# Cross-attention and a mixture-of-experts FFN on one core: the shared FFN of the last five token groups in steps of its own

## The chip, the cores and the metric

One core of one Trainium2 chip runs one program. The metric is the device time in microseconds of one execution of it; lower is better. The time before is 1953.99 us, the median of 3 runs (1952.19 to 1956.04).

## What is computed

```python
# x: 16 x 1024 tokens of 512; context: 16 x 64 x 384; 8 heads of 64; all float32, FFN weights bfloat16
x = x + attention(layernorm(x), ctx) @ Wo + bo           # softmax over 64 context rows, 8 heads
X = layernorm(x).reshape(16384, 512)
scores = sigmoid(X @ gate_w.T)                           # 32 experts
idx = top_k(scores + bias, 4)                            # 4 experts for each token
w = scores[idx] / sum(scores[idx])
# each expert takes its first 512 tokens in order of the tokens; a token beyond is dropped there
ye = (silu(xe @ W1) * (xe @ W3)) @ W2                    # for each expert
out = sum of w * ye over the token's experts
out = out + silu(X @ sw1.T) * (X @ sw3.T) @ sw2.T        # the shared FFN, for every token
x = x + out
```

## The kernel before

The program has two blocks, one after the other, with all five engines joined between them.

**The first block** (`set_up_and_tokens`, L118) goes once over the 16384 tokens, as 128 tiles of 128 tokens. Four tiles are a group (32 groups, numbers 0 to 31). It is one software pipeline written out by hand: every engine runs `step(n)` for n = 0 to 147 (`STEPS`, L56), and each piece of work has a lag (L53 to L55) that says in which step a tile or a group comes to it. The engines meet only through semaphores. For tile t the stages are:

- `XT_LOAD` (n = t+6) and `XT_SPLIT` (t+7): the turned input is loaded and split into a high and a low part, so that products are near float32 (ScalarE L579, GpSimd L658).
- `SCORES` (t+8): TensorE makes the scores of all heads with 12 matmuls into `S_ps` (L374). VectorE takes the maximum (L911) and subtracts it (L917), ScalarE does the exponential (L593), VectorE the sums (L933, L940), GpSimd the division (L664). The scores of the last tile are in step 135.
- `MIX` (t+9): TensorE turns the probabilities (L491), ScalarE and VectorE split them (L585, L924), TensorE makes 12 matmuls into `O_ps` (L390).
- `X1` (t+10): VectorE adds `O_ps` to the tokens (L877) and takes the statistics for the second layernorm. `roots` (L696) is a chain of 13 small VectorE operations (Newton's iteration for 1/sqrt) in each even step, for two tiles at a time.
- `X2` (t+13): ScalarE makes the normalized rows (L568) and their high part in float16 (L573), VectorE the low part (L904), and the SP queue stores the rows and turns both parts with two DMA transposes (L339, L344). `x2_h` and `x2_l` are one buffer each, so the next tile's rows wait until the turned ones have landed (L572, L903).
- `LOGITS` (t+14): 8 small matmuls (L407).

For a group g the stages are `ROUTE` (n = 4g+17, sigmoid and the best 4), `MEMBERS` (4g+18, and on TensorE the ranks, L432), `SLOTS_AT` (4g+19, the slot numbers), `WEIGHTS` (4g+20), `W_STORE` (4g+21). The shared FFN takes `FFN_UP` (4g+17 and 4g+18) and `FFN_DOWN` (4g+19 and 4g+20). An up half c is 16 matmuls into `G_ps` and `U_ps` (L417), a tanh (L619), the gate and the product on VectorE (L754, L759), the high part on ScalarE (L622) and the low part on GpSimd (L651). A down part j is 8 matmuls into the same two banks (L427) and two additions on VectorE (L764). There is one tile `hid` and one pair `ht_h`, `ht_l`.

`TABLE` (n = t+20): GpSimd files the tokens of a tile in the table of slots, with four indirect DMAs (L640) on its own queue, two before and two after its split of `xt` (L653, L660). The second block reads that table, so it can't begin before the last is filed.

```python
file(at(n, TABLE), 0, 2)        # L653
...                             # xt_l (L658)
file(at(n, TABLE), 2, TOP)      # L660
```

Five groups of tokens are held on the chip at a time (`XRING`); the SP queue stores a pair of tiles once its down part is done (L328).

**The second block** (`experts`, L1013) goes over the 32 experts: GpSimd gathers rows by the table (L1087), TensorE turns them and makes the expert's FFN, and GpSimd adds the weighted results into the output (L1099). The change doesn't touch it.

## Time and profile before

| | |
|---|---|
| median of 3 runs | 1953.99 us (1952.19 to 1956.04) |
| the profiled execution | 1951.55 us, its span 1949.7 us |
| first block (to the first instruction of the second) | 1468.38 us |
| second block | 481.3 us |
| TensorE matmuls, weight loads | busy 90% and 64% of the span |
| VectorE, ScalarE, GpSimd | busy 82%, 38%, 64% |

A row of the timeline gives the start in us from the span's start, the duration in us, the engine, the line, the operation, what it writes and reads, and in brackets how long the engine sat idle before it and what released it. The ends of matmuls are modelled. `xr` is the tokens' tile, `x_h` and `x_l` stand for `x2_h` and `x2_l`.

### The profile page before, as it was taken

To read this page: it belongs to the slowest core of one execution; us is meant where nothing else is said; L and a number is where in the kernel's file an instruction comes from. 1 tells how busy PE (TensorE), PEld (TensorE's weight loads), DVE (VectorE), ACT (ScalarE), POOL (GpSimd) and SP (SyncE) were. 2 spreads that over 40 slices of the span, in tenths; PEclk is the share of its full clock that TensorE was granted. 3 is DMA by queue.
4 is the path that set the end of the run, shared out by engine and by line. 5 is a ranking of instruction groups with operands and counts; after the bars stand their busy time and mean duration, and the time that the engine had idled before them with its cause. 6 is when DMAs were issued, how large, how long until landed. Compare 5 with 4: busy or idle time off the path is not lost. (4 is left out here: it accounts for less than half of the span.)

```text
span 1949.7 us, 31394 instructions
## 1 busy us (share of the span) xinstructions
PE 1747.2 (90%) x9424; PEld 1243.4 (64%) x9424; DVE 1591.0 (82%) x4143; ACT 748.8 (38%) x1253; POOL 1241.8 (64%) x1107
## 2 busy tenths in 40 slices
PE   6898899999999999999999999999732999999991
PEld 4775567777777767777776777776411556555551
DVE  5887789999999999999999999999821777676671
ACT  3343334444444444344443444443301444444440
POOL 2235566666676666667666666666675577888864
PEclk8998999999999999999999999999975999999995
DMA  7339987764446464444545444554326799999976
GB/s 210 99 103 101 100 131 131 127 142 119 118 125 145 118 140 132 118 116 132 141 121 139 122 119 121 130 139 111 91 55 204 171 232 218 226 232 220 226 140 78
DMA packets 335195, 275.00 MB, mean 141 GB/s; under 512 B 199858, under 2 KB 242098, under 8 KB 335028
## 3 DMA queue, kind: packets, MB, share of 16 engines
q1 hardware_dynamic: 289972, 203.48, 44.0%
q0 software_dynamic: 45056, 69.52, 18.6%
q8 instruction: 77, 1.26, 0.3%
q14 instruction: 90, 0.74, 0.2%
HBM read 134.07 MB, written 105.25 MB: 123 GB/s over the span
## 5 line engine op out<-in xcount | busy, mean ns | idle before, releaser
L640 POOL DMA_INDIRECT slot_table<-tok,slot x512 | 514.9, 1006 | 125.7 <-issue 121.1
L658 POOL TENSOR_TENSOR xt_l<-xt,xt_h 128x512 fp32r<-128x512 f32 x128 | 166.1, 1298 | 181.8 <-PE S_ps L374 118.5
L1099 POOL DMA_INDIRECT out<-ye,idx x128 | 205.2, 1603 | 88.4 <-issue 37.2
L390 PE MATMUL O_ps<-m_h,pt_h 128*128 128x512 f32 x512 | 217.7, 425 | 33.7 <-issue 30.8
L1251 DVE TENSOR_TENSOR xe_l<-TE_ps,xe_h 128x512 f16<-128x512 f32 x128 | 88.4, 691 | 168.5 <-issue 87.3
L374 PE MATMUL S_ps<-a_h,xt_h 128*128 128x512 f32 x512 | 200.9, 392 | 7.2 <-POOL xt_l L658 7.2
L390 PE MATMUL O_ps<-m_h,pt_l 128*128 128x512 f32 x512 | 201.3, 393 | 0.0
L374 PE MATMUL S_ps<-a_h,xt_l 128*128 128x512 f32 x512 | 201.1, 393 | 0.0
L374 PE MATMUL S_ps<-a_l,xt_h 128*128 128x512 f32 x512 | 200.6, 392 | 0.0
L390 PE MATMUL O_ps<-m_l,pt_h 128*128 128x512 f32 x512 | 200.2, 391 | 0.0
L651 POOL TENSOR_TENSOR ht_l<-hid,ht_h 128x512 fp32r<-128x512 f32 x64 | 82.8, 1294 | 181.2 <-ACT ht_h L622 181.1
L664 POOL TENSOR_TENSOR prob<-prob,rsum 128x512 f32<-128x512 f32 x128 | 134.5, 1051 | 69.0 <-DVE rsum L940 62.1
L593 ACT ACTIVATE prob<-S_ps,rs 128x512 f32<-128x512 f32 x128 | 88.0, 687 | 230.1 <-DVE S_ps L917 211.2
L1087 POOL DMA_INDIRECT rows<-x2aug,idx x128 | 133.4, 1042 | 43.4 <-issue 37.8
L390 PEld LDWEIGHTS O_ps<-m_h,pt_h 128*128 128x128 f32 x512 | 96.5, 188 | 73.5 <-issue 56.2
L585 ACT ACTIVATE pt_h<-TP_ps 128x512 fp32r<-128x512 f32 x128 | 75.9, 593 | 166.0 <-PE TP_ps L491 142.7
L877 DVE TENSOR_TENSOR xr<-xr,O_ps 128x512 f32<-128x512 f32 x128 | 87.1, 681 | 61.2 <-PE O_ps L390 50.9
L622 ACT ACTIVATE ht_h<-hid 128x512 fp32r<-128x512 f32 x64 | 40.5, 633 | 248.4 <-DVE hid L759 245.9
L568 ACT ACTIVATE x<-xr,nb,rs 128x512 f32<-128x512 f32 x128 | 103.5, 809 | 81.9 <-DVE nb L726 59.2
L1151 PE MATMUL TE_ps<-ident_r,rows 128*128 128x128 f32 x512 | 71.0, 265 | 67.0 <-DMA rows<-x2aug,idx 53.9
L1151 PEld LDWEIGHTS TE_ps<-ident_r,rows 128*128 128x128 f32 x512 | 58.6, 145 | 91.8 <-issue 57.5
L374 PEld LDWEIGHTS S_ps<-a_h,xt_h 128*128 128x128 f32 x512 | 97.1, 190 | 29.1 <-issue 6.1
(175 smaller groups left out, 4837.6 us busy)
## 6 DMA issues: line engine op xcount, KB each, us to landing
xt<-in_xT SPq DMA_DIRECT2D x128, 256.0 KB
xr<-in_x SPq DMA_DIRECT2D x64, 512.0 KB, 3.9
x2aug<-x SPq DMA_DIRECT2D x128, 256.0 KB
out<-xr SPq DMA_DIRECT2D x64, 512.0 KB
up_w<-in_w SPq DMA_DIRECT2D x64, 256.0 KB
slot_table<-tok,slot POOLq DMA_INDIRECT x512
down_raw<-in_w SPq DMA_DIRECT2D x32, 256.0 KB
x2t_h<-x_h SPq DMA_TRANSPOSE x128
```

The lines of the kernel that those rows point to most:

```text
L374: last = pe.matmul(S_ps[:, :], left[:, kc, :], right[:, b % 2, kc, :], start=(m == 0), stop=(m == 3 * KD - 1))
L390: last = pe.matmul(O_ps[:, :], left[:, p * P:(p + 1) * P], right[:, b % 2, p, :], start=(m == 0), stop=(m == 3 * PAIRS - 1))
L568: act.activation(x2[:, t % 2, :], x_tile(t), ACT.Identity, bias=nb2[:, q % 2, t % 2:t % 2 + 1], scale=rs[:, (q + LATER) % 2, 1, t % 2:t % ...
L593: act.activation(prob[:, t % 2, :, :], S_ps[:, :].rearrange("p (h j) -> p h j", h=H), ACT.Exp, scale=rs[:, q % 2, 0, t % 2:t % 2 + 1]).the ...
L640: pool.indirect_dma_start(table, bass.IndirectOffsetOnAxis(ap=slot[:, g % 2, i, q:q + 1], axis=0), tok[:, t:t + 1], None, bounds_check=SLO ...
L658: pool.tensor_tensor(xt_l[:, :, :], xt[:, :, :], xt_h[:, t % 2, :, :].bitcast(F32), ALU.subtract).then_inc(xt_lo, 1)
L664: pool.tensor_tensor(prob[:, t % 2, :, :], prob[:, t % 2, :, :], rsum[:, :].unsqueeze(2).to_broadcast([P, H, SKV]), ALU.mult).then_inc(pro ...
L877: dve.tensor_tensor(x_tile(s10), x_tile(s10), O_ps[:, :], ALU.add).then_inc(x1_done, 1)
L1087: pool.indirect_dma_start(rows[:, r, c, :].bitcast(F32), None, x2aug, bass.IndirectOffsetOnAxis(ap=idx[:, e, c:c + 1], axis=0), bounds_che ...
L1099: pool.indirect_dma_start(out, bass.IndirectOffsetOnAxis(ap=idx[:, e, c:c + 1], axis=0), ye[:, e % 4, c, :], None, bounds_check=TOKENS + P ...
L1151: last = pe.transpose(TE_ps[i % 2][:, kc * P:(kc + 1) * P].bitcast(F32R), rows[:, e % RING, i, kc * P:(kc + 1) * P], ident_r[:, :])
L1251: dve.tensor_tensor(xe_l[dst], TE_ps[i % 2][:, :].rearrange("p (c t) -> p c t", c=KD), xe_h[dst], ALU.subtract).then_inc(t_lo, 1)
```

## The change

Nothing of the computation changes. What changes is the step and the place in which pieces are done.

- The shared FFN of groups 27 to 31 (`HELD` = 27) is done in steps 136 to 147, in an order written as a table (`shared_at`). For these groups the low part of the hidden values is made on VectorE (`hidden_lo`), not on GpSimd.
- Rows (`rows_at`): tiles 122 and 123 both in step 135, 124 and 125 in step 137, 126 and 127 in step 138 (before: one tile in each of steps 135 to 140). From tile 125 on an odd tile uses the space of `xt` for its parts. There are two semaphores for the turned parts, by the tile's parity. Logits (`logits_at`): tiles 122 and 123 in step 136, the last four in step 139.
- The last roots are done in step 137 (before 138).
- Routing (`routed_at`): group 29 as before, group 30 one step sooner, group 31 two steps sooner. Filing (`filed_at`): tiles 120 to 127 two in a step, in steps 139 to 142 (before 140 to 147).
- The turned rows of groups 29 to 31 go into the space of `wqc`, `wo_sb`, and `kbd` with `vbd`, which are no longer read by then.
- From step 136 on VectorE runs `late_step`, an order of its own.

```diff
+LAST = TILES - 4
+HELD = GROUPS - 5
+STEPS = LAST + 25
+def rows_at(n):
+    if n < LAST + X2 - 2:
+        return [n - X2] if n >= X2 else []
+    return {LAST + 11: [LAST - 2, LAST - 1], LAST + 13: [LAST, LAST + 1], LAST + 14: [LAST + 2, LAST + 3]}.get(n, [])
+def logits_at(n):
+    if n < LAST + 14:
+        return rows_at(n - 1)
+    return [LAST, LAST + 1, LAST + 2, LAST + 3] if n == LAST + 15 else []
+def filed_at(n):
+    t = n - TABLE
+    normal = [t] if 0 <= t < LAST - 4 else []
+    pair = 2 * (n - LAST - 15)
+    return normal + ([LAST - 4 + pair, LAST - 3 + pair] if 0 <= pair < 8 else [])
+def routed_at(n, lag):
+    for sooner in range(3):
+        g = GROUPS - 3 + sooner
+        if n == 4 * g + lag - sooner:
+            return g
+    g = group_at(n, lag)
+    return g if g is not None and g < GROUPS - 2 else None
+def shared_at(n):
+    if n < LAST + 12:
+        up = [("up", g, c) for c in range(2) for g in (group_at(n, FFN_UP + c),) if g is not None and g < HELD]
+        down = [("down", g, j) for j in range(2) for g in (group_at(n, FFN_DOWN + j),) if g is not None and g < HELD]
+        return up + down
+    u, d, g = "up", "down", HELD
+    return {12: [(u, g, 0)], 13: [(u, g, 1)], 14: [(u, g + 1, 0), (d, g, 0)], 15: [(d, g, 1), (u, g + 1, 1)],
+            16: [(u, g + 2, 0)], 17: [(d, g + 1, 0), (d, g + 1, 1)], 18: [(u, g + 2, 1)],
+            19: [(u, g + 3, 0), (d, g + 2, 0), (d, g + 2, 1)], 20: [(u, g + 3, 1), (u, g + 4, 0)],
+            21: [(d, g + 3, 0), (d, g + 3, 1)], 22: [(u, g + 4, 1)], 23: [(d, g + 4, 0), (d, g + 4, 1)]}.get(n - LAST, [])
...
# TensorE
+                    late = n > LAST + 12
+                    for k, (kind, g, part) in enumerate(shared_at(n)):
+                        if kind == "up":
+                            shared_up(g, part)
+                        else:
+                            shared_down(g, part)
+                        if late and k == 0:
+                            for t in logits_at(n):
+                                logits(t)
+                            if routed_at(n, MEMBERS) is not None:
+                                rank(routed_at(n, MEMBERS))
...
# ScalarE
+                        act.wait_ge(x2_done, t + 1)
+                        after(act, x2_lo, t - 1)
+                        if t == LAST + 1:
+                            act.wait_ge(xt_lo, TILES)
+                        elif t > LAST:
+                            act.wait_ge(x2_turned[t % 2], q * 32)
+                        elif t:
+                            act.wait_ge(x2_turned[(t - 1) % 2], ((t - 1) // 2 + 1) * 32)
+                        act.activation(row_parts(t)[0], x2[:, t % 2, :], ACT.Copy).then_inc(x2_hi, 1)
...
+                    for kind, g, c in shared_at(n):
+                        if kind == "up":
+                            if c and g > HELD:
+                                hidden_hi(g, 0)
+                            act.wait_ge(g_done, TURN_OF["up", g, c] + 1)
                             after(act, ht_lo, g * 2 + c)
                             act.activation(hid[:, :], G_ps[:, :], ACT.Tanh, scale=0.5).then_inc(th_done, 1)
+                            if c or g <= HELD:
+                                hidden_hi(g, c)
...
# GpSimd
+                    for kind, g, c in shared_at(n - 1):
+                        if kind == "up" and g < HELD:
...
# VectorE
+                def late_step(n):
...
+                    if members is not None:
+                        route_mark(members)
+                        route_count(members)
+                        route_before(members)
+                        route_member(members)
+                    for t in rows_at(n):
+                        rows_lo(t)
+                    if slots is not None:
+                        slot_place(slots)
+                        slot_spread(slots)
+                        slot_list(slots)
+                    if weights is not None:
+                        for k in range(5):
+                            weigh_ops(weights, k)
+                    if s10 is not None:
...
+                    for k in range(NEWTON + 1):
+                        if n == LAST + 12:
+                            roots(n, k)
+                        elif n == LAST + 13:
+                            roots(n + 1, k)
+                    if members is not None and members < GROUPS - 1:
+                        slot_over(members)
+                        slot_rank(members)
+                    for kind, g, k in pieces[:1]:
+                        shared_piece(kind, g, k)
+                    if early is not None:
...
+                    if members == GROUPS - 1:
+                        slot_over(members)
+                        slot_rank(members)
+                    for kind, g, k in pieces[1:]:
+                        shared_piece(kind, g, k)
```

## Rows read from the trace of the kernel before

**Rows 1.** The page: the span in 40 equal slices, tenths (busy; granted clock)

```profile
PE   6898899999999999999999999999732999999991
PEclk8998999999999999999999999999975999999995
```

**Rows 2.** Windows: the eleven steps up to 1376.74, and the tail of the block

```profile
1274.00:1376.74 102.74, 97.81 (x516) 70.67 (x515) 99.01 (x279) 39.64 (x68) 68.94 (x63) 0.98 0.43 113
1376.74:1461.40 84.66, 43.43 (x218) 25.25 (x217) 41.89 (x143) 15.58 (x26) 58.86 (x58) 0.81 0.34 78
```

The columns of rows 2 are the window, its length, then busy us (and instructions) of TensorE's matmuls, its weight loads, VectorE, ScalarE and GpSimd, the granted clock, the share of the DMA engines and GB/s.

**Rows 3.** Timeline of GpSimd: filings and what interrupts them, from step 136 on

```profile
1384.61 0.99 POOL L640 DMA_INDIRECT slot_table<-tok,slot  x1 [0.17 <-issue]
...
1401.67 1.26 POOL L651 TENSOR_TENSOR ht_l<-hid,ht_h 128x512 fp32r<-128x512 f32 x1 [7.10 <-ACT ht_h L622]
...
1409.42 1.45 POOL L640 DMA_INDIRECT slot_table<-tok,slot  x1 [0.16 <-issue]
...
1428.32 1.27 POOL L651 TENSOR_TENSOR ht_l<-hid,ht_h 128x512 fp32r<-128x512 f32 x1 [3.34 <-ACT ht_h L622]
...
1460.44 0.98 POOL L640 DMA_INDIRECT slot_table<-tok,slot  x1 [0.30 <-issue]
1468.38 0.20 POOL L1112 MEMSET ident_f<- 128x128 f32 x1 [6.96 <-POOLq L270]
```

**Rows 4.** Timeline of VectorE: step 125's first operation; from step 134 to 136

```profile
1273.08 0.68 DVE L877 TENSOR_TENSOR xr<-xr,O_ps 128x512 f32<-128x512 f32 x1
...
1365.17 0.67 DVE L877 TENSOR_TENSOR xr<-xr,O_ps 128x512 f32<-128x512 f32 x1
...
1365.76 1.04 DVE L713 TENSOR_SCALAR nt<-mv 128x4 f32<-128x4 f32 x1
...
1375.07 0.15 DVE L721 SCALAR_TENSOR_TENSOR nt<-nt 128x4 f32<-128x4 f32 x1
...
1376.74 0.68 DVE L877 TENSOR_TENSOR xr<-xr,O_ps 128x512 f32<-128x512 f32 x1
1377.33 1.15 DVE L851 SCALAR_TENSOR_TENSOR over<-taken,member 128x128 f32<-128x128 f32 x1
...
1379.85 0.69 DVE L911 TENSOR_REDUCE top_s<-S_ps 128x8 f32<-128x512 f32 x1
...
1384.98 0.69 DVE L877 TENSOR_TENSOR xr<-xr,O_ps 128x512 f32<-128x512 f32 x1 [0.21 <-PE O_ps L390]
```

**Rows 5.** Timeline of GpSimd: its low parts of the hidden values beside those steps

```profile
1365.47 1.29 POOL L651 TENSOR_TENSOR ht_l<-hid,ht_h 128x512 fp32r<-128x512 f32 x1 [3.22 <-ACT ht_h L622]
...
1377.04 1.29 POOL L651 TENSOR_TENSOR ht_l<-hid,ht_h 128x512 fp32r<-128x512 f32 x1 [2.52 <-ACT ht_h L622]
```

**Rows 6.** Timeline of ScalarE: the high parts of two tiles, one after the other

```profile
1408.65 0.63 ACT L573 ACTIVATE x_h<-x 128x512 f16<-128x512 f32 x1
...
1413.15 0.63 ACT L573 ACTIVATE x_h<-x 128x512 f16<-128x512 f32 x1 [3.17 <-DMA x2t_l<-x_l]
```

**Rows 7.** Timeline of TensorE: an up half's first matmuls into each bank; a down part's

```profile
1400.52 0.59 PE L417 MATMUL G_ps<-x2t_h,up_sb 128*128 128x512 f16 x1
...
1403.89 0.63 PE L417 MATMUL U_ps<-x2t_h,up_sb 128*128 128x512 f16 x1
...
1413.33 0.48 PE L427 MATMUL G_ps<-down_sb,ht_h 128*128 128x512 f32 x1
...
1414.35 0.39 PE L427 MATMUL U_ps<-down_sb,ht_h 128*128 128x512 f32 x1
```

**Rows 8.** Timeline of VectorE: a long wait in step 137, then the last group's operations

```profile
1396.52 0.69 DVE L877 TENSOR_TENSOR xr<-xr,O_ps 128x512 f32<-128x512 f32 x1 [5.15 <-remote]
...
1430.31 0.69 DVE L754 SCALAR_TENSOR_TENSOR hid<-hid,G_ps 128x512 f32<-128x512 f32 x1 [0.54 <-ACT hid L619]
1431.11 0.69 DVE L759 TENSOR_TENSOR hid<-hid,U_ps 128x512 f32<-128x512 f32 x1
...
1442.21 0.68 DVE L764 SCALAR_TENSOR_TENSOR xr<-U_ps,xr 128x512 f32<-128x512 f32 x1
```

More of the change, by code:

```diff
@@ L322, in step @@
                             load_context(bp)
-                    for k in range(2):
-                        g = group_at(n, OUT + k)
-                        if g is not None:
-                            sp.wait_ge(g_free, g * 4 + 3 + k)
-                            sp.wait_ge(u_free, g * 4 + 3 + k)
+                    for kind, g, k in shared_at(n - 1):
+                        if kind == "down":
+                            sp.wait_ge(g_free, TURN_OF[kind, g, k] + 1)
+                            sp.wait_ge(u_free, TURN_OF[kind, g, k] + 1)
                             sp.dma_start(out_pairs[2 * g + k], x_pair(g, k)).then_inc(out_stored[g % XRING][k], 16)
@@ L502, in step @@
                         turn_probs(t)
[L503 to L505 removed]
+                    late = n > LAST + 12
+                    if not late:
+                        for t in logits_at(n):
+                            logits(t)
                     bp, q = kv_job(n)
@@ L529, in step @@
                         prep_chunk(b, j)
-                    g = group_at(n, MEMBERS)
-                    if g is not None:
+                    g = routed_at(n, MEMBERS)
+                    if g is not None and not late:
                         rank(g)
@@ new lines, in shared_piece @@
+                def shared_piece(kind, g, k):
+                    if kind == "up":
+                        if k and g > HELD:
+                            hidden_lo(g, 0)
+                        gate(g, k)
+                        hidden(g, k)
+                        if k or g == HELD:
+                            hidden_lo(g, k)
+                    else:
+                        residual(g, k, G_ps, g_done, g_free)
+                        residual(g, k, U_ps, u_done, u_free)
+                def late_step(n):
+                    s9, s10 = at(n, MIX), at(n, X1)
+                    early, members = routed_at(n, ROUTE), routed_at(n, MEMBERS)
+                    slots, weights = routed_at(n, SLOTS_AT), routed_at(n, WEIGHTS)
+                    pieces = shared_at(n)
+                    if members is not None:
[3 more added lines that the diff above has]
+                        route_member(members)
+                    for t in rows_at(n):
+                        rows_lo(t)
[7 more added lines that the diff above has]
+                    if s10 is not None:
+                        dve.wait_ge(o_done, s10 + 1)
+                        dve.tensor_tensor(x_tile(s10), x_tile(s10), O_ps[:, :], ALU.add).then_inc(x1_done, 1)
+                        dve.wait_ge(x1_done, s10 + 1)
+                        after(dve, agg2, s10 - 3)
+                        dve.bn_stats(st2[:, s10 % 4, :], x_tile(s10)).then_inc(bn2, 1)
+                        aggregate2(s10)
+                    if s9 is not None:
+                        dve.wait_ge(pt_hi, s9 + 1)
+                        dve.tensor_tensor(pt_l[:, :], TP_ps[:, :], pt_h[:, :].bitcast(F32), ALU.subtract).then_inc(pt_lo, 1)
+                    for k in range(NEWTON + 1):
[9 more added lines that the diff above has]
+                    if early is not None:
+                        route_scores(early)
+                        route_sigmoid(early)
+                        route_bias(early)
+                        route_best(early)
+                        route_cut(early)
+                    if members == GROUPS - 1:
[3 more added lines that the diff above has]
+                        shared_piece(kind, g, k)
@@ L871, in step @@
                     heads = S_ps[:, :].rearrange("p (h j) -> p h j", h=H)
-                    up = [group_at(n, FFN_UP + c) for c in range(2)]
-                    down = [group_at(n, FFN_DOWN + j) for j in range(2)]
+                    pieces = shared_at(n)
                     if s10 is not None:
@@ L947, in step @@
                         route_scores(early)
-                    for c in range(2):
-                        if up[c] is not None:
-                            gate(up[c], c)
                     roots(n, 10)
-                    for j in range(2):
-                        if down[j] is not None:
-                            residual(down[j], j, G_ps, g_done, g_free)
+                    for kind, g, k in pieces[:1]:
+                        if kind == "up":
+                            gate(g, k)
+                        else:
+                            residual(g, k, G_ps, g_done, g_free)
                     roots(n, 11)
@@ L962, in step @@
                         route_bias(early)
-                    for c in range(2):
-                        if up[c] is not None:
-                            hidden(up[c], c)
-                    for j in range(2):
-                        if down[j] is not None:
-                            residual(down[j], j, U_ps, u_done, u_free)
+                    for kind, g, k in pieces[:1]:
+                        if kind == "up":
+                            hidden(g, k)
+                        else:
+                            residual(g, k, U_ps, u_done, u_free)
                     if early is not None:
```

159 lines of the change are left out of this document (88 added, 71 removed).

## The prediction

> **What bounds the kernel now.** I read the page's slices first [rows 1]: TensorE is busy at nine tenths in nearly all slices of the token pass, then falls to 7, 3 and 2 tenths around 1370 to 1500 us, with a lower granted clock. That dip is the only place where work can be filled in. The windows split it [rows 2]: in the steps before 1376.74 VectorE is busy 99.0 of 102.7 us and TensorE 97.8, so both are full; in the tail of the block TensorE has 43 us of work in 85 and VectorE 42. In the tail GpSimd is the engine that ends last [rows 3]: from 1384.61, the start of step 136, it issues 48 filings (L640, 12 tiles of four), one each 0.98 + 0.30 = 1.28 us, and the last starts at 1460.44. The second block begins at 1468.38, 6.96 us after it ended. 48 filings are 61.4 us of 76.8. The rest is four low parts of the hidden values (L651) with their handoffs, 5.0 us, and the waits before two of them, 7.10 and 3.34 us. So before the change the shared FFN costs twice: it fills full steps, and it holds up the filing.
>
> I count from the addition L877 that opens step 135 on VectorE, 1376.74 [rows 4]. Before, filing starts at +7.9, the last filing ends at +84.7 and the second block begins at +91.6.
>
> **Part 1: six up halves and five down parts leave steps 125 to 135.** Each half or part is two large VectorE operations; such an operation takes 0.69 us and the next starts 0.60 after it [rows 4], so 1.2 us of VectorE. TensorE loses more (3.4 us in an up step), but VectorE is the fuller one, so VectorE's share counts. There is a second term. In step 134 the small L713 takes 1.04 us and ends at 1366.80, just when GpSimd's L651 (1365.47 + 1.29) ends; a small operation of that chain otherwise takes 0.15 [rows 4, 5]. L851 of step 135 takes 1.15 and ends by the same 0.15 after the next L651. Without L651 I count back 0.9 for each. By kind of step:
> - first up half (125, 129, 133): 1.2 each, 3.6.
> - second up half (126, 130, 134): 1.2 + 0.9, but in 126 only 0.4 of the wait, 5.8 together.
> - first down part (127, 131): the next addition then waits for `O_ps`, as before step 136 (idle 0.21, rows 4), so the 1.2 is not won; only the 0.9 of L851 is: 1.7.
> - second down part (128, 132): the same loop leaves 0.9 of 1.2: 1.8.
>
> Sum to the start of step 135: 12.9 us of 103.7 (1273.08 to 1376.74, rows 4). Bounds: 0 if the loop scores, maximum, split, mix sets every step, 30 if TensorE did (six times 3.4 and five times 2.04, from two banks of a down part at 1.02 each, rows 7). I take 12.9, since VectorE has hardly a gap in these rows.
>
> **Part 2: step 135 gets two tiles of rows.** Both halves of tile 122 must be turned before `x_h` of tile 123 may be written, and from one to the next is 4.5 us [rows 6]. VectorE has L904 of tile 123 ahead of its maximum (L911), and behind that queue the exponential, the sums and GpSimd's last division, after which the filing starts. `x_h` of 122 at +0.4, of 123 at +5.0, L904 at +5.7, so L911 at +6.3 instead of +3.1 [rows 4]. L851's gain is spent in it. Filing starts at +10.7 instead of +7.9.
>
> **Part 3: the filing.** L651 is gone, but the slots must be ready. Group 29's 16 filings run from +10.7 to +31.2. Group 30's slots come in step 138. VectorE's queue by then, in its order (large operation 0.6, or 0.8 where the next depends on it [rows 8]; a copy on ScalarE 0.63 [rows 6]; a link of the roots about 0.2): weights, x1, statistics and the last split done at +13.8, roots +16.3, group 27's first half with its own low part +19.2, routing of 30 +21.5, members +23.1, rows 124 and 125 +25.0 (one waits for the other's low part), x1 +25.7, statistics +26.8, last roots +29.4, slots over +30.1, second half of 27 +32.9, rows 126 and 127 +35.8, slots of 30 at +37.0. GpSimd idles 5.8 us there and files group 30 until +57.5. Group 31's slots: the four last tiles are turned by about +40.5, logits +42.6, routing +45.4, members +51.1, slots +54.5, in time. Filing ends at +78, where it was +84.7.
>
> **Part 4: the held FFN.** It now goes through one `hid` and one `ht` pair, and this is what I expect to be late next. Group 28's low part is done at +49.6. Group 29 takes until +63.5, since it shares VectorE with group 31's members, slots and weights (4.9 us). After that a group costs 11.2 us: tanh and gate 1.4, four banks of down part at 1.02 [rows 7] 4.1, high and low part 1.4, then the second half's tanh, gate, product, high and low part 4.3. So low parts end at +74.7 and +85.9; the last two down parts with their additions end at +90.8. Before, the last addition ended at 1442.9, +66.2 [rows 8], beside the filing and hidden by it. TensorE's work from group 28's first half on is 8 up halves of 3.4 us and 10 down parts of 2.04, 48 us in 60, so it is not the limit while the clock is high.
>
> **Part 5: the joining of the blocks.** The last store must land and the engines meet. Before that took 6.96 us from the end of the last filing [rows 3], its landing included. For a store of the SP queue no row separates landing and joining; the bounds are 2 and 7, and I take 5.2, nearer to the row. The second block begins at +96.0, against +91.6: 4.4 us later.
>
> **Edits at nothing.** The split semaphore for turned rows, the moved order of gate and roots(10), and the table of turns change neither order nor count of the work before step 125. The stores of five groups (ten of 512 KB) pass in the tail, where the DMA share is 0.34 [rows 2]; if they didn't, the last store would add a few us to part 5. The other buffers are free by step 128.
>
> **Sum.** 12.9 gained, 4.4 given back, and 1 us for TensorE's first matmuls after its longest gap (about 6 us, +24 to +31): after gaps it starts at the lower level, 1.2 GHz, where a bank takes 3.37 us [rows 7], twice what it takes at 2.4. Net 7.5 us. The profiled execution took 1951.55, the median is 1953.99, 2.4 higher; from the median the forecast is 1946.5 us.
>
> **One wait of before is open.** VectorE sat idle 5.15 us in step 137 with nothing named as releaser [rows 8], in a stretch where every engine stood still, and GpSimd's wait of 7.10 holds it. My times of after are without such a wait. If it comes again it costs up to 5 us, so the forecast's own range reaches to 1951.
>
> **Rivals.**
> - *The filing sets the end.* Then FFN handoffs are shorter than I have them and the block ends at +78 + 7.0 = +85, 6.6 us sooner than before: 19.5 us gained, 1934.5. For it: filing was the bound before. Against: it needs the last FFN piece done by about +80, 11 us sooner than worked out. Chance 0.14. One filing of the tail took 1.45 us in place of 0.98 [rows 3]; ten such would change nothing in the forecast. The Trainium skill (SBUF — State Buffer, section SBUF: two separate sides) says that VectorE and GpSimd take a shared port pair as an exclusive lock, and that descriptors of GpSimd's own DMAs wait behind some VectorE operations; by that rule ten low parts moved to VectorE could hold ten filings by 0.69 each, the filing would end near +85, and this rival's time would be 1941.5.
> - *The steps give back only half.* The loop or GpSimd would bound the steps of 9.1 us that I expect (103.7 - 12.9 over ten); GpSimd has four filings, 5.1, and two operations of up to 1.3 in each, 7.7: half of 12.9 gained, 5.4 lost, 1.1 net, 1953. Chance 0.14.
> - *Slower: TensorE at the lower level in the tail.* The mean granted clock of the tail was 0.81 [rows 2], and up halves ran at 3.37 us a bank after gaps of 3 to 5 us. It now hangs on the path that ends last. With all of the 48 us doubled it takes 96 us in a window of 60, 36 us more; with half of it doubled 24 more work against 12 of slack, 12 us more: 1958.5. It turns the sign once more than about 40% of the held matmuls run at 1.2 GHz. Against: the gaps that I work out after +40 are near 2 us at most. Chance 0.12.
> - The forecast as worked out, 1942 to 1951: 0.60.
>
> **Numbers.** 0.2% (3.9 us) is about what a measurement of this kernel can tell from no change; below 1950.1 is faster, above 1957.9 slower. Faster: 0.57 of the forecast's 0.60, 0.14 of the first rival, 0.04 of the second: 0.75. Slower: 0.08 of the clock rival, 0.02 of the second: 0.10. Same: the rest, 0.15. Range 1936 to 1955: it takes in most of both mild rivals and leaves out the filing at its best and the clock at its worst.
>
> **What would show it.** Right: L877 of step 125 to L877 of step 135 about 91 us; a gap of some 5 us on GpSimd between its filings 16 and 17; L651's place taken by a VectorE operation; the last addition L764 some 12 us after the last filing; the second block beginning near 1460. Wrong: steps 126 to 134 as long as before (part 1), the last filing within 5 us of the last addition (part 4), TensorE's held matmuls at 0.63 us (the clock), or a change in the first 1270 us or in the second block's 481 us.

## The result, and the profile after

| | us | |
|---|---|---|
| before, median of 4 runs | 1953.76 | 1952.19 to 1956.04 |
| after, median of 4 runs | 1980.44 | 1977.12 to 1983.44 |
| after / before | 1.0138 | 95% interval 1.0118 to 1.0157 |
| forecast | 1946.5 | 1936 to 1955 |

The changed kernel is 26.7 us slower where 7.5 us faster was forecast. The profiled execution took 1980.39 us, its span 1978.6.

The page of the changed kernel, same two lines as [rows 1]:

```profile
PE   6898899999999999999999999977563999999991
PEclk8999999999999999999999999998886999999996
```

The dip of TensorE around the end of the first block has become wider, five slices at seven tenths or less where there were three. The windows of steps 125 to 134 and of the tail, to the last addition (columns as in [rows 2]):

```profile
1273.75:1368.41 94.66, 74.98 (x384) 58.63 (x384) 83.81 (x260) 36.10 (x60) 63.97 (x61) 0.93 0.40 101
1368.41:1496.83 128.42, 77.89 (x352) 41.33 (x350) 63.88 (x172) 20.65 (x35) 50.56 (x51) 0.84 0.22 62
```

The ten steps did get shorter: 94.7 us, where they took 103.7 [rows 4]. The tail ate it up: in 128 us TensorE has 78 us of work, VectorE 64, GpSimd 51. No engine is the bound. VectorE's timeline (the openings of steps 125, 135, 136 and 137, and the last addition of the held chain):

```profile
1273.75 0.68 DVE L1041 TENSOR_TENSOR xr<-xr,O_ps 128x512 f32<-128x512 f32 x1
...
1368.41 0.69 DVE L1041 TENSOR_TENSOR xr<-xr,O_ps 128x512 f32<-128x512 f32 x1 [1.28 <-issue]
...
1381.89 0.69 DVE L1002 TENSOR_TENSOR xr<-xr,O_ps 128x512 f32<-128x512 f32 x1 [1.88 <-issue]
...
1405.87 0.68 DVE L1002 TENSOR_TENSOR xr<-xr,O_ps 128x512 f32<-128x512 f32 x1
...
1496.14 0.69 DVE L856 SCALAR_TENSOR_TENSOR xr<-U_ps,xr 128x512 f32<-128x512 f32 x1 [0.23 <-PE U_ps L497]
```

GpSimd's timeline (the two gaps in which its filings wait for the slots of the next group, the last filing, the second block; compare [rows 3]). The 48 filings fall into runs of 14, 18 and 16: step 139 also files tiles 120 and 121 of group 30, and their first filings stand ahead of the last two of tile 119.

```profile
1418.17 0.98 POOL L726 DMA_INDIRECT slot_table<-tok,slot  x1 [21.53 <-DVE slot L956]
...
1454.30 0.98 POOL L726 DMA_INDIRECT slot_table<-tok,slot  x1 [13.23 <-DVE slot L956]
...
1474.00 0.98 POOL L726 DMA_INDIRECT slot_table<-tok,slot  x1 [0.30 <-issue]
1500.24 0.21 POOL L1275 MEMSET ident_f<- 128x128 f32 x1 [25.26 <-POOLq L338]
```

Counted from the opening of step 135, as in the prediction, the last addition ends at +128.4 and the second block begins at +131.8. The balance of the two profiled executions: 9.0 us gained in the steps, 0.7 lost before them, 131.8 - 91.6 = 40.2 lost in the tail, 3.0 gained in the second block (478.36 for 481.32): 28.9 us, the difference of the spans.

What the engines waited for is in the list of waits (waiting engine, tile and line, releaser: us in total, times, longest), here those that end on nothing that the profile names:

```profile
ACT lexp L688 <- remote: 28.1, 2, 22.2
ACT hid L708 <- remote: 11.7, 3, 4.9
ACT ht_h L625 <- remote: 11.0, 1, 11.0
DVE hid L846 <- remote: 5.4, 2, 3.7
DVE xr L856 <- remote: 5.0, 3, 2.8
```

All of these wait, directly or one step further, for TensorE. Its timeline, and below it ScalarE's, show how late its work is seen. The last logits matmul of group 31 is recorded from 1422.82 to 1423.00, the up half behind it to 1429.48; the exponential that needs nothing but the logits starts at 1438.18, and the tanh of that up half at 1443.85. TensorE, which waits for the gate behind that tanh, stands idle for 15.75 us. That up half is slow itself: it takes 6.6 us, with gaps that the profile puts to nothing (one of 1.04 us is shown), where it takes 3.6 us on chip C below. So TensorE's own stream of matmuls is disturbed in such a stretch too, and not only what the others see of it.

```profile
1422.82 0.18 PE L477 MATMUL R_ps<-gate_sb,vbd 128*128 128x32 bf16 x1
...
1425.39 0.38 PE L487 MATMUL G_ps<-x2t_l,up_sb 128*128 128x512 f16 x1 [1.04 <-issue]
...
1429.10 0.38 PE L487 MATMUL U_ps<-x2t_l,up_sb 128*128 128x512 f16 x1
1445.22 1.03 PE L487 MATMUL G_ps<-wqc,up_sb 128*128 128x512 f16 x2 [15.75 <-DVE hid L841]
```

```profile
1388.88 0.28 ACT L688 ACTIVATE lexp<-R_ps 128x128 f32<-128x128 f32 x1 [5.96 <-remote]
1393.81 0.60 ACT L708 ACTIVATE hid<-G_ps 128x512 f32<-128x512 f32 x1 [4.65 <-remote]
...
1438.18 0.28 ACT L688 ACTIVATE lexp<-R_ps 128x128 f32<-128x128 f32 x1 [22.17 <-remote]
...
1443.85 0.60 ACT L708 ACTIVATE hid<-G_ps 128x512 f32<-128x512 f32 x1 [4.87 <-remote]
```

I call this a late signal: the time from the recorded end of a matmul to the moment at which another engine goes on. There are three such stretches, 1383 to 1399, 1423 to 1444 and 1464 to 1477. In all but the last 2 to 3 us of each GpSimd files without a break, one filing about every 1.28 us. No wait of this kind begins where it doesn't file (1396.6 to 1418.2, 1441.1 to 1454.3, after 1475.0), and the last wait of each stretch ends 2.1, 2.8 and 2.1 us after the run of filings. The Trainium skill (Perfetto Trace Analysis, section Per-engine timelines) says that a matmul's recorded end is an estimate and that its semaphore goes out only after PSUM has acknowledged the write; it gives no time for that. The trace alone therefore doesn't tell whether the write or the signal was held up.

### The profile page after: what moved, and what is told of

Read it like the earlier page. It is cut to its first block and busy times, and to the rows that moved or that the text cites. A ratio compares the mean times of both kernels' runs of the same rounds, so it can differ in the third digit from the quotient of the medians.

```text
span 1978.6 us, 31396 instructions
## 1 busy us (share of the span) xinstructions
PE 1758.7 (89%) x9424; PEld 1245.6 (63%) x9424; DVE 1599.4 (81%) x4153; ACT 749.3 (38%) x1253; POOL 1227.0 (62%) x1097
## 5 line engine op out<-in xcount | busy, mean ns | idle before, releaser
L1262 POOL DMA_INDIRECT out<-ye,idx x128 | 203.7, 1592 | 86.9 <-issue 37.8
L736 POOL TENSOR_TENSOR ht_l<-hid,ht_h 128x512 fp32r<-128x512 f32 x54 | 70.0, 1297 | 152.6 <-ACT ht_h L625 152.6
L651 ACT ACTIVATE x<-xr,nb,rs 128x512 f32<-128x512 f32 x128 | 103.6, 809 | 89.5 <-DVE nb L813 69.2
L1328 PE MATMUL YE_ps<-down_w,he_h 128*128 128x512 f32 x256 | 110.4, 431 | 2.6 <-DVE he_l L1408 2.0
L1370 ACT ACTIVATE xe_h<-TE_ps 128x512 f16<-128x512 f32 x128 | 75.3, 589 | 98.7 <-PE TE_ps L1314 63.3
```

The lines of the kernel that those rows point to most:

```text
L651: act.activation(x2[:, t % 2, :], x_tile(t), ACT.Identity, bias=nb2[:, q % 2, t % 2:t % 2 + 1], scale=rs[:, (q + LATER) % 2, 1, t % 2:t % ...
L1262: pool.indirect_dma_start(out, bass.IndirectOffsetOnAxis(ap=idx[:, e, c:c + 1], axis=0), ye[:, e % 4, c, :], None, bounds_check=TOKENS + P ...
L1328: last = pe.matmul(YE_ps[i % 2][:, :], part[:, e % 2, c, i * P:(i + 1) * P], down_w[:, e % 2, c, :], start=(n == 0), stop=(n == 2 * KI - 1))
```

## The experiments

**Theory 1**: GpSimd's filings, when nothing comes between them, hold TensorE's signals back, and the chain of the held FFN now depends on them. **Theory 2**: the order of the tail itself (bursts of logits, one `hid`, a low clock) makes it long, whoever files. The runs fell on five chips, and the chip turned out to matter, so the table names them A to E; which chip the first two profiles come from isn't on record. All times in the tail are counted from the addition that opens step 135.

| run (chip) | ratio to before, 95% | last addition ends | last filing starts | second block begins |
|---|---|---|---|---|
| before, first profile | | +66.2 | +83.7 | +91.6 |
| after, first profile | 1.0138 | +128.4 | +105.6 | +131.8 |
| no late filings (A) | 0.9974 (0.9958 to 0.9989) | +91.4 | none | +95.1 |
| before, no late filings (A) | 0.9861 (0.9828 to 0.9894) | +58.4 | none | +62.2 |
| broken runs (A) | 1.0105 (1.0064 to 1.0147) | +107.6 | +115.0 | +123.0 |
| TensorE kept busy (A) | 1.0138 (1.0095 to 1.0181) | +127.6 | +102.5 | +131.0 |
| tiny rests (B) | 0.9992 (0.9975 to 1.0008) | +91.6 | +83.6 | +95.0 |
| tiny rests, waited for (B) | 1.0043 (1.0027 to 1.0060) | +93.1 | +94.6 | +102.6 |
| rest every four (B) | 1.0061 (1.0042 to 1.0081) | +100.8 | +98.5 | +107.6 |
| fewer signals (B) | 1.0003 (0.9983 to 1.0023) | +92.8 | +81.7 | +96.2 |
| changed kernel again (C) | 0.9998 (0.9982 to 1.0014) | +93.3 | +82.2 | +96.7 |
| kernel before again (C) | 0.9995 (0.9978 to 1.0011) | +60.5 | +78.0 | +85.9 |
| fewer signals (C) | 0.9997 (0.9981 to 1.0014) | +92.0 | +82.3 | +95.4 |
| tiny rests, fewer signals, busy (C) | 0.9977 (0.9958 to 0.9996) | +92.3 | +84.3 | +95.7 |
| tiny rests (D) | 1.0124 (1.0092 to 1.0157) | +121.8 | +103.1 | +125.2 |
| fewer signals (D) | 1.0182 (1.0155 to 1.0208) | +132.2 | +109.2 | +135.6 |
| tiny rests, fewer signals, busy (D) | 1.0093 (1.0056 to 1.0129) | +117.4 | +97.2 | +120.9 |
| wait for landing (E) | 1.0038 (1.0019 to 1.0058) | +94.2 | +97.5 | +105.5 |
| wait for landing, busy (E) | 1.0009 (0.9991 to 1.0026) | +94.6 | +97.5 | +105.4 |
| tiny rests, waited for (E) | 0.9999 (0.9977 to 1.0020) | +94.2 | +93.8 | +103.1 |

The kernel before took, in median, 1951.0 us on A, 1932.9 on B, 1928.7 on C, 1946.7 on D and 1948.6 on E.

**No late filings.**

```diff
-                    for t in filed_at(n):
+                    filed = filed_at(n) if n < LAST + 12 else []
+                    for t in filed:
                         file(t, 0, 2)
```

> The changed kernel without the 48 filings that GpSimd issues from step 136 on; the tokens of tiles 116 to 127 aren't filed for the second block. Theory 1 (TensorE's completion signals come late while GpSimd files without a break, and the held chain waits for them): no wait of the tail ends on a late signal of TensorE, the last addition comes about 91 us after the L1041 addition that opens step 135 instead of 128, and the second block begins with it: about 1943 us, 37 less than the changed kernel. Theory 2 (the order itself, with bursts of logits, one hidden buffer and a low clock, makes the tail long, whoever files): the last addition stays at 120 to 128 us, 1972 to 1980 us.

Measured 1944.5 us. The last addition ends at +91.4, where the prediction had +90.8, and the tail has no wait on remote. With the filings it ends at +127.6 on the same chip (TensorE kept busy, below). VectorE's and GpSimd's timelines:

```profile
1449.37 0.69 DVE L857 SCALAR_TENSOR_TENSOR xr<-U_ps,xr 128x512 f32<-128x512 f32 x1 [0.24 <-PE U_ps L497]
```

```profile
1453.76 0.20 POOL L1276 MEMSET ident_f<- 128x128 f32 x1 [84.66 <-POOLq L338]
```

So the filing delays an addition that doesn't need it by 36 us on chip A, or by 37 us against the first profile. Theory 2 falls: the order is the same.

**The same in the kernel before** (`file` gets no tile from step 136 on).

> The kernel before without the filings of its steps from 136 on; the tokens of tiles 116 to 127 aren't filed for the second block. Theory 1: the 5.15 us that VectorE waits at 1391 us for TensorE's signal goes, the last addition comes 58 to 62 us after the opening of step 135 instead of 66, and the second block, no longer held by filing, begins about 5 us behind it: 1927 to 1931 us. Theory 2: the 5.15 us stays, the last addition stays at 66, about 1934 us.

Measured 1920.8 us; the 5.15 us wait [rows 8] is gone, step 137 opens 6.3 us after step 136 instead of 11.5, and the second block begins at +62.2. Theory 1 was right on the wait. The block began 29 us sooner, 2 us more than the 23 to 27 expected.

**Broken runs.** After every second filing from step 136 on:

```diff
+    pool.tensor_tensor(xt_l[:, :, :], xt_h[:, 0, :, :].bitcast(F32), xt_h[:, 1, :, :].bitcast(F32),
+                       ALU.subtract).then_inc(xt_lo, 1)
+    pool.wait_ge(xt_lo, TILES + rests[0])
```

> The changed kernel with an unneeded GpSimd operation of 1.3 us (a subtraction of two tiles of scratch) after every second filing from step 136 on, as the steps before have one. All that was computed still is. Theory 1, if it is the unbroken run that holds signals back: waits on late signals fall to under 3 us each, the last addition comes 91 to 105 us after the opening of step 135 although filing takes 24 times some 1.4 us longer (34 us); filing then ends about 112 us after it and sets the end: 1962 to 1968 us. If filings beside matmuls hold signals back whether or not the run is broken: last addition at 125 us or later, 1980 us or over. Theory 2: last addition at 128, 1980 us.

Measured 1968.5 us, and +107.6 where up to +105 was expected. No wait on remote is left in the tail, though all 48 filings stand beside the matmuls. GpSimd's timeline shows the pause, from the end at 1409.42 to 1411.50:

```profile
1408.44 0.98 POOL L726 DMA_INDIRECT slot_table<-tok,slot  x1 [0.30 <-issue]
1409.43 1.29 POOL L733 TENSOR_TENSOR xt_l<-xt_h 128x512 fp32r<-128x512 f32 x1
1411.50 0.99 POOL L726 DMA_INDIRECT slot_table<-tok,slot  x1 [0.77 <-POOL xt_l L733]
```

It is the unbroken run that does it, not a filing beside a matmul; chip A shows this with a pause of 2.1 us. The last addition is at +107.6, 16 us above the run without filings, and that isn't late signals: beside the 24 operations of 1.3 us VectorE needs 76.1 us for the same 172 instructions of the tail for which it needs 63.4 without filings. The run with a rest every four, on a chip without late signals, lies between (12 such operations, 70.1 us, +100.8; +91.6 with one-column ones).

**TensorE kept busy.** In steps 125 to 135:

```diff
+    for _ in range(8 if (n - LAST) % 4 in (1, 2) else 6):
+        pe.matmul(G_ps[:, :], earlier[:, :], up_sb[:, 0, :], start=True, stop=True)
```

> The changed kernel with 6 to 8 matmuls whose result isn't used in each of steps 125 to 135, so that TensorE has as much to do there as before. If the lower granted clock that the removed matmuls brought cost the 4 us that part 1 fell short, the granted clock stays at 2.4 GHz in these steps, step 135 opens 10 to 13 us earlier than before (now 8.3) and the time falls by 2 to 4 us, to about 1977 us. If it cost nothing: steps as now, or up to 5 us longer by the added matmuls, 1980 to 1986 us. Neither touches the late signals of the tail.

Windows of steps 125 to 134 of this run, and of the changed kernel from 1353 to 1381:

```profile
1262.93:1354.44 91.51, 84.96 (x458) 61.76 (x457) 82.68 (x261) 36.44 (x60) 64.27 (x61) 0.98 0.41 104
```

```profile
1353.00:1381.00 28.00, 20.71 (x88) 16.61 (x89) 21.11 (x69) 8.05 (x13) 15.91 (x16) 0.76 0.29 72
```

Ten steps take 91.5 us with 72 needless matmuls more and 94.7 without them. The granted clock is 0.98 in place of 0.93: with 75 us of work in 94.7, parts of these steps run at 1.2 GHz (the window above begins in them and reaches to the end of step 135), and that takes back 3.2 us. The tail is as long as in the changed kernel (+127.6), so the late signals are on chip A too. The time, 1972.7 us, has the ratio of the changed kernel on the first chip; the changed kernel itself didn't run on A, but the other edits leave the work of these ten steps as it is, so all profiles can be compared. In the thirteen profiles without these matmuls the ten steps take 94.5 to 94.7 us at a granted clock of 0.93, 95.2 to 95.4 at 0.91 and 96.2 to 96.8 at 0.88 or 0.89; in the four with them 91.4 to 92.3 at 0.98. On E, where a pair differs in nothing else (the two runs that wait for landing), they take 6.7 us off the median, 1948.7 for 1955.4.

**Rests of other kinds, and fewer signals, on chip B.** The rests stand after every second filing (every fourth in the third run). The tiny rest subtracts one column, and only the second run waits for it. In the run of fewer signals TensorE gives one signal for four tiles of logits:

```diff
-                    last.then_inc(logits_done, 1)
+                    if t < LAST - 4:
+                        last.then_inc(logits_done, 1)
+                    elif t % 4 == 3:
+                        last.then_inc(logits_done, 4)
```

> The changed kernel with a GpSimd subtraction of one column after every second filing from step 136 on, and no wait behind it. If any other instruction between the filings lets TensorE's signals through: no wait of over 2 us on a late signal, last addition 91 to 100 us after the opening of step 135, filing ends about 95 us after it (24 times some 0.4 us more), the second block begins at 97 to 104: 1945 to 1952 us, 28 to 35 less than the changed kernel. If it must be a pause of GpSimd or of its queue of some 2 us, as the 0.78 us wait and the 1.3 us operation of the run with broken runs made: last addition at 120 to 128, 1972 to 1980 us.

> As the run before, but GpSimd also waits for the one-column subtraction to be complete before it files on (0.78 us in the run with broken runs). If a wait is what lets the signals through: last addition 91 to 100 us after the opening of step 135, filing 24 times 1 us longer, its end at 100 to 105, 1953 to 1958 us. If the length of the pause counts and 1 us is too short: last addition at 115 us or later, 1968 us or over.

> As the run with broken runs (1.3 us operation and wait), but after every fourth filing, 12 instead of 24 rests. If one rest lets all signals through that have piled up: waits on late signals of 1 to 5 us each, last addition 95 to 108 us after the opening of step 135, filing ends at about 100, 1950 to 1960 us. If each rest lets through only one or two signals: last addition at 115 us or later, 1968 us or over.

> The changed kernel with one signal of TensorE for the four tiles of logits of groups 30 and 31 instead of four, at the same place in its order. If each signal of TensorE costs about 4 filings (5 us) while GpSimd files on, the stall that now ends at 1438 us loses three signals of 3 to 6 us and the first stall one of 5: last addition 108 to 116 us after the opening of step 135, 1961 to 1969 us. If the signals are held until the filing pauses, whatever their number: last addition at 125 to 128, 1977 to 1980 us.

The first, second and fourth came within 2 us of the run without filings, the fourth below what any theory allowed. With the kernel before at 1932.9 us, 18 to 21 us less than seen so far, the chip was suspect, and these four runs say nothing on what lets signals through.

**The two kernels again, on chip C.**

> The changed kernel itself once more, on the chip of the three runs beside it. The kernel before took 1951 us on the chip of the first four experiments and 1933 on that of the next four, so those four may owe a part to the chip. If the late signals are there on every chip: 1.3 to 1.4% slower than the kernel before, last addition 125 to 131 us after the opening of step 135. If the chip of the last four runs shows none: 0 to 0.3% from the kernel before, last addition at 91 to 93.

> The kernel before, for its profile on the same chip. With late signals: VectorE waits about 5 us for one in step 137 and the second block begins 91 us after the opening of step 135. Without: no such wait, and filing, which waits for slots that come 5 us sooner or not at all later, lets the second block begin 84 to 91 us after it.

> One signal for the four tiles of logits of groups 30 and 31, again, beside the changed kernel. Fewer signals are the cause: 1.2 to 1.4% faster than the changed kernel on this chip, whatever the chip. The chip was the cause: as the changed kernel within 0.3%; or, where this chip shows late signals, last addition 108 to 116 us after the opening of step 135.

> The changed kernel with three additions: the one-column subtraction on GpSimd after every second filing, one signal for four tiles of logits in groups 30 and 31, and the 6 to 8 unneeded matmuls in steps 125 to 135. If signals were all that was wrong with the tail and the clock with the steps before it: last addition 91 to 93 us after the opening of step 135, the second block at 95 to 97, and the opening 3 to 4 us earlier; against the kernel before 91.6 - 96 + 8.3 + 3.5 = 7 us faster, 0.35%. If the signals are late in it all the same: slower than the kernel before.

The chip, or what goes with it, was the cause. Here the changed kernel equals the one before, and its whole trace has not one wait on remote. The run with tiny rests, fewer signals and a busy TensorE is faster than the kernel before by 4 us by the ratio (0.9977) and by 2 by the medians, where 7 was expected. The window of the changed kernel's tail, up to the start of its last addition:

```profile
1361.06:1453.70 92.64, 74.19 (x352) 42.35 (x350) 63.29 (x172) 20.54 (x35) 51.75 (x51) 0.89 0.31 88
```

The same logits and exponential on TensorE's and ScalarE's timelines:

```profile
1404.76 0.18 PE L477 MATMUL R_ps<-gate_sb,vbd 128*128 128x32 bf16 x1
```

```profile
1404.97 0.28 ACT L688 ACTIVATE lexp<-R_ps 128x128 f32<-128x128 f32 x1 [7.01 <-PE R_ps L477]
```

GpSimd's timeline with the one gap left, and VectorE's with the last addition:

```profile
1400.11 0.98 POOL L726 DMA_INDIRECT slot_table<-tok,slot  x1 [10.32 <-DVE slot L956]
...
1443.24 1.46 POOL L726 DMA_INDIRECT slot_table<-tok,slot  x1 [0.30 <-issue]
1457.74 0.20 POOL L1275 MEMSET ident_f<- 128x128 f32 x1 [13.04 <-POOLq L338]
```

```profile
1453.64 0.69 DVE L856 SCALAR_TENSOR_TENSOR xr<-U_ps,xr 128x512 f32<-128x512 f32 x1 [0.62 <-PE U_ps L497]
```

The logits of group 31 end at 1404.94 and the exponential starts at 1404.97; in the first profile 15.2 us lay between the same two. The filings are as dense in both, mostly 0.98 + 0.30 us. The kernel before on this chip has no 5 us wait either, and its second block begins at +85.9 (GpSimd's timeline):

```profile
1455.33 0.20 POOL L1112 MEMSET ident_f<- 128x128 f32 x1 [6.95 <-POOLq L270]
```

The second block, which nobody changed, sorts the chips as well: 467.5 to 471.9 us in the eight profiles of B and C, 478.4 to 484.4 in the twelve of the first chip, A, D and E. Those twelve have waits on remote in it (at `xe_h` 12.3 us in the first profile of the kernel before), the eight have none.

**Again on chips with late signals.** Chip D:

> The changed kernel with the one-column GpSimd subtraction, not waited for, after every second filing from step 136 on, once more, to meet a chip with late signals; the kernel before tells which it is (1950 us or more with them, about 1930 without). On a chip with late signals: if any instruction between filings lets them through, last addition 91 to 100 us after the opening of step 135 and a ratio to the kernel before of 0.996 to 1.001; if only a pause of some 2 us does, last addition at 115 us or later and a ratio of 1.007 to 1.014. On a chip without them: last addition at 91 and 0.999, as it was.

> The changed kernel with one signal for the four tiles of logits of groups 30 and 31, for the same reason. On a chip with late signals: if each signal costs 3 to 6 us while GpSimd files, last addition 108 to 116 us after the opening of step 135 and a ratio of 1.003 to 1.008; if signals are held until filing pauses, 125 to 128 and 1.012 to 1.014. On a chip without them: last addition at 91 and 1.000, as it was.

> The changed kernel with the one-column rests, the fewer signals and the unneeded matmuls together. On a chip with late signals: if tiny rests let them through, last addition 91 to 100 us after the opening of step 135, and the version beats the kernel before there too, ratio 0.993 to 0.998; if they don't, ratio 1.000 to 1.008. On a chip without them: 0.998, as it was.

GpSimd's timeline of the tiny rests, and ScalarE's long wait for the logits in the run of tiny rests and in that of fewer signals:

```profile
1376.82 0.99 POOL L726 DMA_INDIRECT slot_table<-tok,slot  x1 [0.30 <-issue]
1377.83 0.20 POOL L736 TENSOR_TENSOR xt_l<-xt_h 128x1 fp32r<-128x1 f32 x1
1378.19 1.00 POOL L726 DMA_INDIRECT slot_table<-tok,slot  x1 [0.16 <-issue]
```

```profile
1422.13 0.28 ACT L688 ACTIVATE lexp<-R_ps 128x128 f32<-128x128 f32 x1 [17.53 <-remote]
```

```profile
1431.01 0.28 ACT L691 ACTIVATE lexp<-R_ps 128x128 f32<-128x128 f32 x1 [27.28 <-remote]
```

Fewer signals gain nothing (+132.2, ratio 1.0182, both beyond what was expected even of signals held until the filing pauses): the price isn't one for each signal. The exponential goes at 1431.0, 20 us after its logits and 2 us after a run of filings that ends at 1429. With tiny rests, 0.38 us from the end of one filing to the start of the next where it is 0.30 without, the last addition comes 10 us sooner than with fewer signals on the same chip, and 7 us of 37 sooner than in the first profile. The changed kernel itself didn't run on D.

Chip E:

> The changed kernel, with GpSimd waiting after every fourth filing from step 136 on until its filings have landed: pauses without any GpSimd operation, as long as the landing takes, not measured so far, 1 to 3 us by the pauses tried. The kernel before tells the kind of chip (1947 us or more with late signals, about 1930 without). With late signals: if a pause of the filing lets them through, last addition 93 to 108 us after the opening of step 135 (121 with tiny rests, 131 with fewer signals, 107 with 1.3 us operations and waits after every two), filing ends at 90 to 105, ratio to the kernel before 1.000 to 1.007; if it is the GpSimd operation, not the pause, 118 or later and 1.010 or over. Without late signals: last addition at 91 to 93, ratio 1.000 to 1.006 by the longer filing.

> The same with the unneeded matmuls in steps 125 to 135, which open step 135 3 to 4 us earlier. With late signals, if the pauses let them through: 0.997 to 1.005 of the kernel before; else 1.008 or over. Without late signals: 0.997 to 1.004.

> The changed kernel with the one-column subtraction and a wait for it after every second filing, once more, for a chip with late signals. If a pause of about 1 us is enough there: last addition 92 to 100 us after the opening of step 135, ratio 1.002 to 1.006. If the late signals shrink with the length of the pause (121 us with no wait, 107 us with 2.07 us): last addition 110 to 118, ratio 1.006 to 1.011. If only the 2 us pause does anything: 120 to 125, 1.011 to 1.014. Without late signals: last addition at 92, 1.004.

GpSimd's timelines: of the wait for landing (after every fourth filing), then of the tiny rest that is waited for (after every second):

```profile
1382.34 0.98 POOL L726 DMA_INDIRECT slot_table<-tok,slot  x1 [1.93 <-DMA slot_table<-tok,slot]
```

```profile
1383.82 0.99 POOL L726 DMA_INDIRECT slot_table<-tok,slot  x1 [0.30 <-issue]
1384.83 0.20 POOL L736 TENSOR_TENSOR xt_l<-xt_h 128x1 fp32r<-128x1 f32 x1
1385.81 1.01 POOL L726 DMA_INDIRECT slot_table<-tok,slot  x1 [0.77 <-issue]
```

Both bring the last addition to +94.2, about as on chips without late signals. If E has them, a pause is what lets the signals through, with or without an operation in it: 1.0 us after two filings is enough, 1.9 us after four nearly so (one wait of 1.5 us on remote is left), while 0.38 us isn't on D. That E has late signals is inferred: no run without a pause was made there. It rests on its second block (478.7 to 480.5 us, and 9.3 us of waits on remote at `xe_h` in the last run), on the 1948.6 us of the kernel before, and on that one wait. What is shown on one chip, with and without, is the 2.1 us pause on A.

## Why the prediction was wrong

**Part 1, ten steps without FFN.** Forecast 12.9 us, measured 9.0, and 9.2 on C (95.4 for 104.5). The count of VectorE operations was right: with TensorE kept busy the ten steps take 91.5 us on A and 92.3 on C, 12.1 and 12.2 less than the 103.6 and 104.5 of the old order on the same chips. The term that was missing is the clock, 3.2 us between these two profiles and 2.2 to 5.4 over all that have the same steps. I had charged the lower level 1 us, in the tail, and nothing to the steps that lose a quarter of TensorE's work.

**Part 2 and 3.** The maximum after the two tiles of rows was forecast at +6.3 and came at +6.2 (1374.57 in the first profile). On C filing starts at +10.6 (forecast +10.7), slots of 30 are ready at +38.2 (+37.0), of 31 at +55.3 (+54.5). Filing ends at +83.6, not +78, for three reasons. It resumes at +39.1, 2 us later. I had misread my own order: 14 filings can go before the slots of group 30, not 16, so 34 are left and not 32, which is 2.6 us. And single ones take up to 1.46 us, 1.3 us in all. The rule of the Trainium skill that the prediction cited (SBUF — State Buffer, section SBUF: two separate sides) would have made it +85. That is close, but by chance: a filing that starts less than 0.6 us after one of the moved low parts (L851) does take longer, by 0.17 to 0.48 us, but that happens four times here and not ten, and never costs 0.69. All of this is hidden, since the FFN ends later, as forecast.

**Part 4, the chain of the held FFN.** On C low parts end at +50.8, +64.4, +75.6 and +86.9 (forecast +49.6, +63.5, +74.7, +85.9) and the last addition at +93.3 (+90.8); +91.4 without filings. Part 5 took 3.4 us, not 5.2, so the second block begins at +96.7 on C, and +96.0 was forecast. On the chip of the result it begins at +131.8.

**The step that failed** is the last before the rivals, "One wait of before is open". The 5.15 us wait of the kernel before [rows 8] was a late signal: it goes without filings, and on C. TensorE's timeline of the kernel before has the last matmul that this addition needs, with an end at 1391.29, 5.2 us before the addition starts:

```profile
1390.90 0.39 PE L390 MATMUL O_ps<-m_h,pt_l 128*128 128x512 f32 x1
```

I saw that nothing explained it and then capped its return at its own size, "up to 5 us". It was one signal of TensorE that happened to be needed in an unbroken run of filings. The change takes L651 off GpSimd, which had broken these runs, and puts the last logits and the whole held FFN, each step of which needs a signal of TensorE, beside them. Their lateness sums up, and delays the slots and with them the next filings: GpSimd waits 21.5 and 13.2 us for slots, where it waits 10.3 us and not at all on C. It cost 128.4 - 91.4 = 37.0 us, against 5. That GpSimd could hold up more than its own queue had no place in the sum.

**The sum on a chip without late signals.** There the kernel before has no such wait and its second block begins 5.7 us sooner (+85.9 for +91.6). With that, 9.2 gained and 96.7 - 85.9 = 10.8 given back make 1.6 us slower; measured 0.9998, which is 0 with 3 us to either side. So even without late signals the forecast of 7.5 us faster is gone: 3.7 is lost in the steps, most of it to the clock, 5.7 to a wait that I had left standing in before alone, and 0.7 to the chain; the 1 us that I had charged to the clock in the tail comes off.

**The rivals.** The filing didn't set the end. The steps gave back 70%, not half. TensorE at the lower level in the tail doesn't carry the result: on C the mean clock of the tail is 0.89, with 0.84 in the slow one, and the chain on C ended 2.5 us after its forecast. No rival named the mechanism. The "slower" chance of 0.10 stood on the wrong one.

**A version that beats both?** On C tiny rests, fewer signals and a busy TensorE together take 0.9977 of the kernel before; on D the same kernel takes 1.0093. On E two paced versions equal the kernel before, 0.9999 and 1.0009. None beats it on every chip. Waited tiny rests with a busy TensorE weren't run; from the runs above I estimate 3 us less than 0.9999 on E.

## What to carry to other kernels

A wait that no engine and no DMA explains has no price yet: find what stands beside it (here an unbroken run of GpSimd's indirect DMAs) and count how often the changed kernel will need a signal in such a stretch, instead of taking its length as a bound. Where GpSimd issues DMAs in a row beside a chain that goes through TensorE, try a pause of 1 to 2 us after two of them: it costs that engine its length, and with it no late signal was left on A or E. Run the kernel on more than one chip before the comparison is believed. Taking work off a full TensorE lowered its granted clock here; some needless matmuls won 2 to 5 us back.

## What the runs showed of the hardware

- On the first chip and on A and D, signals of TensorE came 2 to 20 us late while GpSimd issued one indirect DMA about every 1.28 us, and on the first chip one up half of TensorE took 6.6 us for 3.6; ScalarE's and VectorE's signals went on time to each other in the same stretches. A pause of 2.1 us after two issues removed it on A; on E none was there with pauses of 1.0 us. B and C showed none of it in the tail, with the same instructions at the same pace; the kernel before runs there in 1929 to 1933 us, elsewhere in 1947 to 1954.
- Whether a chip, the core on it that a program gets or a condition of it makes the two kinds stays open; each kind held for all the runs of a set. Whether the signal or the write into PSUM ahead of it is late stays open too, and so does whether GpSimd's issuing does it or the writes that these DMAs make: no run separates the two.
- The wait from the last of four filings to its landing was 1.87 to 3.8 us long.
- An indirect DMA of GpSimd (0.98 us) that started 0.1 to 0.4 us after a VectorE subtraction with both inputs in SBUF (L851) took 1.15 to 1.46 us, on B, C and in the first profile alike.
